# Preparing the query tiles one block ahead instead of two in a fused attention and feed-forward kernel

## What is computed

```python
xn = _layernorm(x)                         # eps 1e-5
# attention, fed with xn
k, v = split(xn @ Wkv)                     # one k and one v of 64 for all heads
q = (layer_norm(xn) @ Wq)                  # 16 heads of 64
k, v = concat(null_k, k), concat(null_v, v)
q = l2norm(q) * q_scale;  k = l2norm(k) * k_scale
sim = q @ k.T * 8                          # causal, first 64 rows see 64 columns
attn_out = softmax(sim) @ v @ Wout
# feed-forward, also fed with xn
Wt = clip(round(W / (mean(abs(W)) + 1e-5)), -1, 1)      # for W1 and for W2
ffn_out = relu(xn @ Wt1.T + b1) @ Wt2.T + b2
y = x + attn_out + ffn_out
```

## Time and profile before

| | us |
|---|---|
| median of 2 runs | 1975.21 (1964.07 to 1986.35) |
| profiled execution, its own time | 1961.71 |
| span of its slowest core (core 6) | 1960.2 |
| spans of the eight cores | 1934.1 to 1960.2 |
| prologue (tiles 0 to 7), from 61 to 263 | 202 |
| block 0, from 263 to 427 | 164 |
| block 1, from 427 to 681 | 254 |
| block 2, from 681 to 892 | 211 |
| block 3, from 892 to 1173 | 281 |
| weight loads and last part, from 1173 | 787 |

### The profile page before, as it was taken

The page is one execution under the profiler, slowest core; times in us unless marked ns, Lnnn a source line. Parts: engine busy times, 40 slices in busy tenths (PEclk is TensorE's granted clock), DMA queues, the critical chain, the costliest instruction groups (busy, mean ns, idle before and its releaser), DMA issues.

```text
span 1960.2 us, 20133 instructions; the slowest of 8 cores (1934.1 to 1960.2 us)
## 1 busy us (share of the span) xinstructions
PE 1507.6 (77%) x5609; PEld 572.2 (29%) x5609; DVE 467.0 (24%) x1616; ACT 612.5 (31%) x1123; POOL 145.9 (7%) x217
## 2 busy tenths in 40 slices
PE   0222266887769999999999980798989898988986
PEld 0111122222222233333333330443434333433432
DVE  1454446554443222121222110100100110011000
ACT  0000023343334568777767750021002001200210
POOL 2000000000000111111111110000000000000000
PEclk9766656565655678887989885699599969977998
DMA  4122244544533445555555649012131232123123
GB/s 111 44 55 54 57 122 125 158 141 133 140 102 95 100 104 132 126 119 122 127 113 130 124 92 272 13 43 81 49 118 43 82 97 70 43 92 102 44 70 118
DMA packets 184492, 194.20 MB, mean 99 GB/s; under 512 B 114590, under 2 KB 152480, under 8 KB 183360
## 3 DMA queue, kind: packets, MB, share of 16 engines
q10 hardware_dynamic: 42336, 97.00, 16.4%
q1 hardware_dynamic: 126240, 51.40, 12.1%
q0 software_dynamic: 15808, 44.52, 8.6%
HBM read 139.26 MB, written 29.49 MB: 86 GB/s over the span
## 4 chain that ended last, share of the span: by engine, by line
PE 53%; DMA 24%; DVE 10%; issue 7%; ACT 2%; ACTq 2%; POOL 1%; DVEq 0%; SPq 0%; POOLq 0%
PE psim L1127 11%; PE pav L897 6%; PE psim L1151 6%; PE pwork L1151 6%; DMA wtout<-wqbf 6%; PE pwork L863 5%; PE psim L816 5%; PE psim L1042 3%; DMA ktok<-kvT_sb 3%; DMA w2qt<-wtout 3%; DMA xbufB<-x 2%; DMA wstage<-W 2%; DMA w2ring<-w2qt 2%; DVE qtmp L747 2%; DVE qhat L762 2%
## 5 line engine op out<-in xcount | busy, mean ns | idle before, releaser
L829 ACT ACTIVATE attnT<-psim,negC 128x512 bf16<-128x512 f32 (+3 forms) x518 | 296.5, 618 | 175.0 <-PE psim L816 52.0
L897 PE MATMUL pav<-attnT,v_sb 128*64 128x512 bf16 (+3 forms) x640 | 269.7, 425 | 22.1 <-DVE outunT L915 22.1
L1142 ACT ACTIVATE h1full<-psim,b_sb 128x512 bf16<-128x512 f32 x128 | 86.7, 687 | 638.0 <-PE psim L1127 568.6
L1127 PE MATMUL psim<-xnTg,W1B 128*128 128x512 bf16 x1024 | 240.6, 379 | 16.3 <-ACT h1full L1142 16.3
L816 PE MATMUL psim<-qhatT,khsT 64*128 64x512 bf16 (+3 forms) x518 | 209.2, 404 | 31.9 <-ACT attnT L829 26.5
L863 PE MATMUL pwork<-attnT,dind 128*2 128x512 bf16 (+3 forms) x640 | 176.8, 438 | 0.0
L1151 PE MATMUL psim<-w2ring,h1full 128*128 128x512 bf16 x512 | 170.5, 418 | 5.3 <-DMA w2ring<-w2qt 5.2
L1151 PE MATMUL pwork<-w2ring,h1full 128*128 128x512 bf16 x512 | 171.2, 419 | 0.0
L518 DVE TENSOR_SCALAR wqbf<-wstage 128x512 bf16<-128x512 f32 x128 | 55.0, 430 | 393.9 <-DMA wtout<-wqbf 223.1
L1127 PEld LDWEIGHTS psim<-xnTg,W1B 128*128 128x128 bf16 x1024 | 99.0, 98 | 139.9 <-issue 22.8
L1042 PE MATMUL psim<-invdenT,indic 2*128 2x128 f32 x256 | 70.5, 414 | 79.9 <-DMA w2ring<-w2qt 55.5
(11 more groups left out here) (142 smaller groups left out, 1195.3 us busy)
## 6 DMA issues: line engine op xcount, KB each, us to landing
wstage<-W ACTq DMA_DIRECT2D x128, 512.0 KB, 4.1
w2ring<-w2qt SPq DMA_DIRECT2D x32, 512.0 KB, 3.8
w2ring<-w2qt ACTq DMA_DIRECT2D x32, 512.0 KB, 3.4
xbufA<-x POOLq DMA_DIRECT2D x16, 512.0 KB, 4.8
w1qt<-wtout POOLq DMA_DIRECT2D x32, 256.0 KB, 3.2
w2qt<-wtout POOLq DMA_DIRECT2D x32, 256.0 KB, 3.2
xbufB<-x POOLq DMA_DIRECT2D x32, 256.0 KB, 3.7
wstage<-Wq ACTq DMA_DIRECT2D x8, 512.0 KB, 4.5
```

The lines of the kernel that those rows point to most:

```text
L829: ts_=ts_: s.activation(attnT[:, ts_, c, j0 * 128:j0 * 128 + w], ring_ap2(slot, 0, 128, 0, w), AF.Exp, bias=negC[:, 0:1]),
L897: w=w: t.matmul(pav[po:po + 64, j0 * 128:j0 * 128 + w], v_sb[:, c, :], attnT[:, ts_, c, j0 * 128:j0 * 128 + w], start=(c == 0), stop=False ...
L1127: sp=sp: tt.matmul(PM1[rot][:, 0:TW], W1B[:, c, fc * 128:(fc + 1) * 128], xnTg[:, sp, c, :], start=(c == 0), stop=(c == ND - 1)),
L1142: s.activation(h1full[:, fc, 0:TW], PM1[rot][:, 0:TW], AF.Relu, bias=b1_sb[:, fc:fc + 1]),
```

## The change

The prologue prepares one block of tiles instead of two, and each block of heads carries the tiles of the next block instead of the one after it. Block 0 now carries tiles 4 to 7, block 1 tiles 8 to 11, block 2 tiles 12 to 15, and block 3 none.

```diff
-    for i0 in range(min(2 * BQ, NT)):
+    for i0 in range(min(BQ, NT)):
         for s in stage0_steps(i0):
             s()
...
         steps_next = []
-        if (B4 + 2) * BQ < NT:
-            for i2 in range((B4 + 2) * BQ, (B4 + 3) * BQ):
+        if (B4 + 1) * BQ < NT:
+            for i2 in range((B4 + 1) * BQ, (B4 + 2) * BQ):
                 steps_next += stage0_steps(i2)
```

## The result

The changed kernel takes 1938.63 us (median of 11 runs, 1933.56 to 2013.68), the kernel before 1963.54 (10 runs, 1949.32 to 1986.35). The ratio is 0.9887 [0.9861, 0.9912]: 22 us or 1.1% less. It leaves out executions in which the cores of a die show a lower clock and a longer time, as in the one of 2013.68 us; the two medians as they stand differ by 25. The gain is small, inside the 2% of which the prediction spoke, but the interval leaves out 1. The forecast was 1928, with a range of 1894 to 1962.

What follows compares the result with a forecast made beforehand. The prologue was taken as bound by latency, block 2 by PE. From the profiled 1961.7 us, -100.6 (prologue) + 6.5 (start of block 0) + 60 (block 2) gave 1927.6, forecast as 1928, range 1894 to 1962.

Steps and rivals of the forecast that it cites:

- prologue less start of block 0: Four tiles leave the prologue, -100.6 us; the first scores wait for the last prologue tile's `qhatT`, +6.5 us.
- blocks 0 and 1, turns: Blocks 0 and 1 keep 40 equal-cost steps; turns between blocks have 11 us of cover for `qhatT`: 0 us.
- block 2: Four tiles enter block 2: 42 us for their work and waits plus 18 for the clock, 60 us longer.
- PE's added work: In block 2, each tile's projections, k and v matmuls and small transpose take PE 5.4 us; 22 for four.
- waits: In block 2, per tile: 2.7 us after `s_kv`, 1.5 after `s_qproj`, 1 for a quantisation step behind the statistics.
- Rival D: A turn between blocks waits, costing up to 3 x 10 us, total 1958; chance 0.23 together with Rival B.
- Rival A: Preparation almost disappears in block 2, which grows by about 28 us, total 1896; chance 0.21.
- Rival C: The clock does not come back in block 2, which grows by 145 us, total 2013; chance 0.06.
- Rival B: SP's transpose queue becomes the bound; block 2 grows by 86 us, total 1954; chance 0.23 together with Rival D.
- the clock term of block 2: PE's waits in block 2 bring six further lower-clock heads of 6.0 us, less three natural ones: 18 us.
- three natural ones: Three lower-clock heads already wholly inside block 2 before the change, 6.0 us each, taken to coincide with new ones.
- The 30 us worked out for it: Block 2's clock cost if all eight waits end in a slow head: 48 - 18 = 30 us, total 1940.

Runs made afterwards that it cites:

- e8: Changed kernel with tiles cut into twelve steps instead of ten, emitted singly over the chunks of the first 14 heads: 1861.32 us, ratio to before 0.9472.
- e1: Changed kernel without the 24 quantisation transposes in block 2: 1927.93 us, ratio to before 0.9821.
- e5: Changed kernel without the four norm activations of tiles 12 to 15, which reuse tile 11's norms: 1926.21 us, ratio to before 0.982.
- e6n: Changed kernel with block 2's quantisation steps moved to each head's last six chunks and tiles 12 to 15's norm activations left out: 1941.14 us.
- e2: Changed kernel with the same ten uncut steps emitted singly, spread over the chunks of the first 14 heads: 1884.02 us, ratio to before 0.9612.
- e10: Changed kernel with each group of three uncut steps put behind the middle chunk of the head's scores: 1946.54 us, ratio to before 0.9952.
- e4: Changed kernel with block 2's four tiles moved into block 1, six steps behind each head there: 1988.09 us, ratio to before 1.0137.
- e3: Changed kernel with each group of up to three steps emitted ahead of the head's denominator run instead of behind it: 1977.95 us, ratio to before 1.0058.

## Why the prediction was right, and where it was not

In numbers, by its own terms:

| term | forecast | measured |
|---|---|---|
| prologue less start of block 0 | -100.6 + 6.5 = -94.1 | -93.3 (first exponential) |
| blocks 0 and 1, turns | 0 | -0.7 |
| block 2 | +60 | +74 |
| of it PE's added work | 22 | 21 (21.7 by e8) |
| of it waits | 20 | 22 (25 on the slowest cores) |
| of it lower clock | 18 | 31 (28 on the slowest cores) |
| block 3 | 0 | -3.2 |
| last part | 0 | -7, within the spread of the cores |
| whole profiled execution | -34 | -26.7 |

**The prologue** came out within 1 us, because it is one serial chain whose pace can be read off, and because the place where the chain is given back (the first score behind the last `qhatT`) was counted along it.

**The total** is nearer than its parts. Block 2 grew by 14 us more than forecast, while block 3 and the last part, for which the forecast had 0, came out 10 us shorter. That the profiled execution came out 7 us from the sum (1935.0 against 1927.6) is in part luck.

**Rival D**, a turn that waits, did not come: the two blocks in front of the turns are unchanged to 1 us. **Rival A** (28 us) fell with the 74 us of block 2; its evidence, came from a place where the clock was low anyway, so that it could not show what a lost clock costs. **Rival C** (145 us) fell, since heads at the full clock stand between the slow ones (the 11.1 us head above). **Rival B** has a true core of 10 us (e1), but its sign, VectorE's wait for `wtout` far above 67 us, is missing: that wait became shorter. (GpSimd's wait for the same transposes grew from 117.6 to 203.3 us; e1 shows what taking them out is worth.)

**The step that was mis-sized is the clock term of block 2.** I took six further slow heads of 6.0 us, less three natural ones, 18 us. Eleven of sixteen heads were above 17 us on core 4, and the matmuls that were there before grew by 28 there, by 31 in the mean of the cores. The waits were 22 to 25 in place of 20. The page of the Trainium skill that I had weighed, "TensorE: Matmul & The Clock Gate", section "HAM oscillation — how this bites in real kernels", says that stalls between bursts of matmuls throttle the engine again at every burst. The 30 us worked out for it make a block 2 of 42 + 30 = 72 us, nearer than my 60 to the 74 measured. The trace agrees in that drawn-out heads became the rule; block 2 of e5 and of e8, set side by side in the last section, shows that the share of stalls alone does not set the number.

**The mechanism behind the waits was only half right.** I priced each ScalarE wait by itself: 2.7 and 1.5 us per tile, 17 for four. Taking both activations out gave 7 (e5), and the other wait that came in their place gave no net gain when removed as well (e6n). The sum of the waits was near all the same; the parts that I added up were not separate costs, so that is luck in part. What e2 and e10 show in their place is one cost of the group of steps: spread out, the same steps cost 28 us less in block 2.

e2's gain in block 1 (35 us by the means of the cores) is mostly wait: PE's idle time fell from 47.0 to 25.0 us, its busy time from 202.5 to 189.2, at a clock of 0.72 instead of 0.65. In block 2 it is the other way round: idle from 29.1 to 17.4, busy from 253.4 to 237.9.

What stays open: why e4's group of six costs 30 us per tile, above the serial 25.2, beyond the one wait shown; and by what way a group of steps brings the lower clock with it.

## What to carry to other kernels

Preparation that is bound by latency is well moved off a prologue, but its price in the new place depends on how it is placed: a few dependent steps in a row cost 74 us in block 2 here, and the same steps emitted singly between independent work 46, cut finer as well 38, of which 22 are their own matmuls. Removing one wait of such a chain told little here (e5, e6n); change the spacing first, and price the chain as one. Whenever a step is moved, look at what frees a buffer behind it on the same engine (in e3 a copy that came late made TensorE wait 23.5 us in block 2 instead of 2.5).

## What was not expected of the hardware

The granted clock does not follow PE's idle time alone. In block 2 of e5 PE was idle 25.0 of 280.0 us at a clock of 0.76 (core 0):

```profile
600.80:880.80 280.00, 254.97 (x849) 81.92 (x848) 95.33 (x374) 159.22 (x284) 31.06 (x39) 0.76 0.46 107
```

In e8 it was idle 21.9 of 247.3 us, the same share (8.9%), at 0.86 (row above). The longest waits are alike too, 3.4 us in e5 and 4.6 in e8. From PE's waits in block 2 of e5, then of e8 (us in total, times, longest):

```profile
PE psim L822 <- ACT attnT L835: 13.3, 5, 3.4
...
PE ptrb L643 <- DVE mu2b L641: 6.1, 2, 3.2
```

```profile
PE ptrb L643 <- DVE mu2b L641: 9.0, 2, 4.6
```

One thing that differs is where the idle time lies: mostly ahead of scores in e5, ahead of value matmuls and the small transpose in e8. But e6n has most of its idle time at the same two places as e8 (11.5 and 5.8 of 26.6 us), and its clock is 0.75, so that does not decide it. Nor does the share of idle time: e2 on core 4 has 16.0 of 259.0 us, less than e8, at 0.80 (rows above). What decides it, no run shows. It is worth 30 us of PE's busy time in block 2 (255.0 against 225.4, for the same matmuls).
